# Context products of a cross-attention: one value matrix against 256 tokens in four column groups, and a 0/1 matrix back to token rows

## The reference

```python
q = split(x @ Wq + bq); k = split(ctx @ Wk + bk); v = split(ctx @ Wv + bv)   # 16 heads of 8 features
scores = q @ k.T / sqrt(8)            # 77 columns for each token and head
keep the 32 largest scores of each row; w = softmax over what is kept
out = concat(w @ v) @ Wo + bo
```

## Time and profile before

| what | us |
|---|---|
| runs | 611.84, 613.88, 619.55 |
| profiled execution, its own time | 621.08 |
| its span from first to last instruction | 619.3 |
| TE busy | 542.8 |
| VectorE busy | 409.9 |
| ScalarE busy | 294.3 |
| GpSimd busy | 223.5 |
| mean granted clock of TE, as a share of full | 0.964 |

### The profile page before, as it was taken

One profiled execution on the slowest core, in us unless ns is written; L12 is line 12 of the kernel. 1 busy time (PEld: TensorE's weight loads), 2 busy tenths in 40 slices (PEclk: granted clock), 3 DMA queues, 4 the chain that ended last, 5 costly groups with the idle time before them and its releaser, 6 DMA issues.

```text
span 619.3 us, 12159 instructions
## 1 busy us (share of the span) xinstructions
PE 542.8 (88%) x3982; PEld 425.0 (69%) x3982; DVE 409.9 (66%) x2225; ACT 294.3 (48%) x726; POOL 223.5 (36%) x227
## 2 busy tenths in 40 slices
PE   4888679997899899989998889968799988999997
PEld 2565347875667566768667656657577877989997
DVE  3566765533544598776697998876768889534643
ACT  2342314324775576663763645545575555222221
POOL 4016830002433464562552655542623432420000
PEclk9997989998999999998999979889899999789999
DMA  4500102404000000000000000003600000000000
GB/s 132 177 1 14 45 20 68 130 25 153 2 2 1 0 2 2 2 1 1 2 2 1 2 3 2 1 1 103 190 11 11 13 19 19 22 23 1 26 1 10
DMA packets 23050, 19.17 MB, mean 31 GB/s; under 512 B 2048, under 2 KB 18508, under 8 KB 22989
## 3 DMA queue, kind: packets, MB, share of 16 engines
q1 hardware_dynamic: 22477, 17.36, 9.2%
q0 software_dynamic: 512, 1.05, 0.6%
HBM read 15.38 MB, written 3.01 MB: 30 GB/s over the span
## 4 chain that ended last, share of the span: by engine, by line
PE 60%; DVE 23%; ACT 10%; issue 4%; POOL 1%; another core or an unknown queue 1%; DMA 1%; DVEq 0%; ACTq 0%
PE ps L1793 51%; DVE wk L1165 6%; DVE top L1155 4%; PE ps L2183 3%; DVE nmax L1101 3%; ACT prT L1562 2%; DVE sel_mem L994 2%; ACT w_mem L1555 2%; PE ps L2245 1%; ACT pr L1555 1%; ACT w_lo L1681 1%; DVE xn L1128 1%; PE ps L2366 1%; DVE sel_mem L1289 1%; PE ps L1805 1%
## 5 line engine op out<-in xcount | busy, mean ns | idle before, releaser
L1165 DVE MATCH_REPLACE8 wk<-top,wk 128x77 f32<-128x77 f32 x384 | 80.6, 225 | 0.8 <-issue 0.8
L1101 DVE TENSOR_REDUCE nmax<-ps 128x2 f32<-128x256 f32 (+1 forms) x64 | 51.2, 821 | 41.3 <-PE ps L1793 39.5
L687 POOL TENSOR_TENSOR w_mem<-w_mem,rinv 128x256 f32<-128x256 f32 (+3 forms) x44 | 53.3, 1223 | 52.7 <-DVE rinv L1107 52.2
L1289 DVE TENSOR_TENSOR sel_mem<-gr,ps 128x512 f32<-128x512 f32 x47 | 32.3, 687 | 53.5 <-ACT gr L1736 52.6
L1155 DVE MAX8 top<-wk 128x8 f32<-128x77 f32 x384 | 58.3, 225 | 2.1 <-issue 0.9
L1736 ACT ACTIVATE gr<-ps 128x512 f32<-128x512 f32 x47 | 28.1, 598 | 61.2 <-PE ps L1793 61.2
L1793 PE MATMUL ps<-cat_mem 64*128 64x512 f32 (+7 forms) x272 | 54.4, 480 | 1.5 <-ACT cat_mem L1539 1.5
L716 POOL TENSOR_SCALAR wk<-wk 128x616 f32<-128x616 f32 x16 | 28.1, 1755 | 59.4 <-DVEq L1169 59.2
L1555 ACT ACTIVATE w_mem<-ps,nmax 128x128 f32<-128x128 f32 (+3 forms) x88 | 44.5, 519 | 10.0 <-DVE nmax L1101 9.9
L1793 PE MATMUL ps<-prT,cat_mem 128*64 128x128 f32 x640 | 44.2, 287 | 0.0
L611 POOL TENSOR_TENSOR rstd<-var_eps,minus_half 128x4 f32<-128x4 f32 x8 | 8.2, 1026 | 97.8 <-DVE var_eps L831 97.7
(11 more groups left out here) (346 smaller groups left out, 1369.0 us busy)
## 6 DMA issues: line engine op xcount, KB each, us to landing
w_mem<-in_L_ffn_W_dram SPq DMA_DIRECT2D x12, 256.0 KB, 3.1
f_mem<-in_L_ffn_Wg_dram SPq DMA_DIRECT2D x8, 256.0 KB, 2.7
f_mem<-in_L_ffn_Wu_dram SPq DMA_DIRECT2D x8, 256.0 KB, 3.0
f_mem<-in_L_ffn_Wd_dram SPq DMA_DIRECT2D x8, 256.0 KB, 3.6
sel_mem<-in_L_ffn_W_dram SPq DMA_DIRECT2D x4, 256.0 KB, 4.0
xs_dram<-zero SPq DMA_DIRECT2D x1, 960.0 KB, 6.1
ys_dram<-f_mem SPq DMA_DIRECT2D x15, 64.0 KB, 1.5
xs<-xs_dram SPq DMA_DIRECT2D x3, 256.0 KB, 3.1
```

Source lines behind the costliest of these rows:

```text
L687: pool.tensor_tensor(pr[s][:, :, at:at + n], pr[s][:, :, at:at + n], rinv[:, i % 8, :].unsqueeze(2).to_broadcast([P, 2, n]), ALU.mult)\
L1101: dve.tensor_reduce(nmax[:, i % 8, :], ps[:, 2 * s:2 * s + 2, at:at + (c + 1) * P], X, ALU.max, negate=True).then_inc(nmax_ready, 1)
L1165: dve.match_replace(wk[q][:, t, h, :], top[q][:, t, h, 8 * r:8 * r + 8], src[:, t, h, :], GONE).then_inc(top_step, 1)
L1289: dve.tensor_tensor(hg[s][:, :], gr[s][:, :], ps[:, 2 * s + 1, :], ALU.mult)\
```

## The change

`context` puts the head's values on the stationary side: for each of the four heads one product, with 32 columns of `vh` (9 that count and 23 that belong to the next heads, or to a tail filled with ones) as the stationary operand and all 256 tokens of `pkT` as the moving one. The four outputs go to partitions 0 to 31, 32 to 63, 64 to 95 and 96 to 127 of the same 256 columns. A piece's result thus has its features on the partitions. ScalarE copies all 256 columns, to `cxT`. A new step `context_rows` brings a block's four pieces back to token rows: for each half and piece one product with `cxT` as the stationary operand and `pick9`, a 0/1 matrix of 36 columns which picks 9 of each 32 partitions, as the moving one. VectorE then normalises straight from PSUM. The fillers ahead of `context_T` are gone. `pkT` becomes one tile, and its two copies write strided. Two semaphores are merged. The transposes of the exponentials stay at their places in the order of every engine.

```diff
-        vh = sb("vh", [NC, B, HX, DX + 1])
+        vh_mem = sb("vh", [NC, B * HX * (DX + 1) + 32 - DX - 1])
+        vh = vh_mem[:, 0:B * HX * (DX + 1)].rearrange("p (b h d) -> p b h d", b=B, h=HX)
+        pick9 = sb("pick9", [P, 4 * (DX + 1)])
...
-        pkT = [part(sel_mem, t * S, 4, P)[0:NC] for t in range(2)]
-        cx = part(sel_mem, 2 * S, 2, 4, 8 * (DX + 1))
+        pkT = part(sel_mem, 0, 4, 2 * P)[0:NC]
...
+        cxT = [cxT_even, cxT_one, cxT_even, part(fn_flat[2], 0, 4, 2 * P)]
+        cn = [cn_first, cn_first] + [part(fn_flat[2], 2 * S, 2, D)] * 2
...
-            def context_norm(k):
-                dve.wait_ge(cx_ready, 4 * (k + 1))
+            def context_norm(k, bank):
+                dve.wait_ge(rows_cx_ps, k + 1)
...
-                act.activation(cx[:, n // 4 % 2, n % 4, :], ps[:, bank, 0:8 * (DX + 1)], ACT.Copy).then_inc(cx_ready, 1)
+                if n % 4 == 0 and n >= 8:
+                    act.wait_ge(rows_cx_ps, n // 4 - 1)
+                act.activation(cxT[n // 4][:, n % 4, :], ps[:, bank, 0:2 * P], ACT.Copy).then_inc(cx_ready, 1)
...
                 pe.wait_ge(pkT_ready, 2 * n + 2)
-                for t in range(2):
-                    for h in range(4):
-                        at = (4 * t + h) * (DX + 1)
-                        last = mm(ps[:, bank, at:at + DX + 1], pkT[t][:, h, :], vh[:, n // 8, 4 * (n % 4) + h, :])
+                for h in range(4):
+                    at = (HX * (n // 8) + 4 * (n % 4) + h) * (DX + 1)
+                    last = mm(ps[32 * h:32 * h + 32, bank, 0:2 * P], vh_mem[:, at:at + 32], pkT[:, h, :])
                 last.then_inc(cx_ps, 1)
                 return ((cx_ready, n + 1),)
+
+            def context_rows(k, bank, *free):
+                for signal, count in free:
+                    pe.wait_ge(signal, count)
+                pe.wait_ge(cx_ready, 4 * (k + 1))
+                n9 = 4 * (DX + 1)
+                for t in range(2):
+                    for n in range(4):
+                        last = mm(ps[:, bank, (4 * t + n) * n9:(4 * t + n + 1) * n9], cxT[k][:, n, t * P:(t + 1) * P],
+                                  pick9[:, :])
+                last.then_inc(rows_cx_ps, 1)
+                return ((cn_ready, 2 * (k + 1)),)
 
             def context_T(k, out_c, *free):
...
-                if k < 2:
-                    keep_busy(7, 4)
                 pe.wait_ge(cn_ready, 2 * (k + 1))
...
+                for k in range(2):
+                    if U == OUT[k]:
+                        seven = context_rows(k, 7, *seven)
...
+                if j == 3:
+                    four = context_rows(2, 4, *four)
...
+                if i == 4:
+                    four = context_rows(3, 4, *four)
```

More of the change, by code:

```diff
@@ L497, in decoder @@
         yg = part(fn_flat[1], 0, 2 * TB, D)
+        cxT_even = part(sel_mem, 2 * S, 4, 2 * P)
+        cxT = [cxT_even, cxT_one, cxT_even, part(fn_flat[2], 0, 4, 2 * P)]
+        cn = [cn_first, cn_first] + [part(fn_flat[2], 2 * S, 2, D)] * 2
         SCALE0 = float(D) ** -0.5
@@ L632, in _ @@
                 pool.memset(cum[q][:, 0:E], 0.0).then_inc(pool_step, own.up())
-            pool.memset(vh[:, :, :, :], 1.0).then_inc(pool_step, own.up())
+            pool.memset(vh_mem[:, :], 1.0).then_inc(pool_step, own.up())
+            pool.memset(pick9[:, :], 0.0).then_inc(pool_step, own.up())
             pool.iota(slots[:, :], pattern=[[1, P]], base=0, channel_multiplier=0,
@@ L643, in _ @@
             keep_where(later_t16[:, :], [[-1, P]], 0, 1, NEG)
+            by_head = pick9[:, :].rearrange("p (h d) -> p h d", h=4)
+            pool.affine_select(out=by_head, in_=by_head, compare_op=ALU.not_equal, fill=1.0, base=0,
+                               pattern=[[-32, 4], [-1, DX + 1]], channel_multiplier=1).then_inc(pool_step, own.up())
             by_e = same_e16[:, :].rearrange("p (e j) -> p e j", e=E)
@@ L1603, in weights_T @@
                     act.wait_ge(cx_ps, n)
-                act.activation(pkT[t][:, :, :], tiles(bank)[0:NC], ACT.Copy).then_inc(pkT_ready, 1)
+                act.activation(pkT[:, :, t * P:(t + 1) * P], tiles(bank)[0:NC], ACT.Copy).then_inc(pkT_ready, 1)
             def tokens_high(k):
```

39 lines of the change are left out of this document (20 added, 19 removed).

## The result

The changed kernel takes 619.67 us (median of 20 runs, 614.59 to 623.84), the kernel before 613.60 (20 runs, 611.72 to 619.55). The ratio is 1.0073, 95% interval 1.0050 to 1.0096: slower by about 4.5 us, where 6.9 us faster was forecast. The sign was wrong, beyond what the measurement leaves open.

What follows compares the result with a forecast made beforehand. TE was taken as the bound in most stretches, VectorE in others. Gains 3.9 + 4.0 + 1.6 + 4.55 less losses 1.8 + 2.0 + 0.9 + 2.0 + 0.5 gave 6.85 us: 607 us from the median 613.88, range 598 to 621.

Steps and rivals of the forecast that it cites:

- contexts 0, 1, 2 and the clock behind 2: Self-attention: shorter contexts on TE gain 3.9 us; full clock after the third of them gains 1.7 us.
- unit 36: Block 0's `context_rows` in self-attention delays TE's transposes and next scores; fillers gone give part back: 0.9 us lost.
- the clock behind context 5: Self-attention: of a 6.8 us low-clock stretch, only the last 4 or so count; full clock gains 2.0 us.
- unit 44: Block 1's `context_rows`: score product waits for VectorE's normalisation; fillers gone and full clock help: 2.0 us lost, bounds 1 and 3.
- contexts 9, 10, 11: Weight preparation and tokens: TE's time counts, each context falling from 1.71 to 0.70 us to the next start.
- step 3: Block 2's `context_rows` among the experts: 1.7 us of products plus 0.3, the down product covering 1.14: 2.0 us lost.
- context 14: Tokens: this context runs at low clock, 2.97 us; the new one takes twice 0.70: 1.6 us gained.
- context 15, block 3, clock there: Last context shortened from 1.71 to 0.70 us; `context_rows` at step 4 loses 1.8; half the clock's 1.7, 0.85, gained.
- first rival: In the contexts, the four column groups run one after another, so contexts give 0.5 not 9.5: 616 us, chance 0.10.
- second rival: The clock doesn't care for thin products, so the 4.55 us of clock gain go: 611.5 us, chance 0.14.
- third rival: `context_rows` brings low clock at its four places, costing 10 us, and the 4.55 gain goes: 621.6 us, chance 0.13.
- clock term: Removing thin products keeps full clock after three contexts: 4.55 us gained, bounds 0 and 6.8.

Runs made afterwards that it cites:

- e0: The kernel before, unchanged, run again for a second reference trace: 614.39 us, ratio 0.998.
- e6: The kernel before with each 9-column context product widened to 126 columns, the same nine repeated: 613.02 us, ratio 0.9944.
- e2: The changed kernel with one product of 288 columns in place of the sixteen records of `context_rows`, waits kept: 609.49 us, ratio 0.9897.
- e14: The changed kernel with the ways back of blocks 0 and 1 moved later, block 2's left in place: 610.32 us, ratio 0.9931.
- e8: e4 with block 1 (contexts 4 to 7) put back in the old form: 606.00 us, ratio 0.9869.
- e11: The changed kernel with only block 2's products moved, from step 3 to the end of the step before: 623.14 us, ratio 1.0119.
- e12: The changed kernel with only block 0's way back moved late: products at the end of unit 36, normalisation and turn one unit later: 610.25 us, ratio 0.9930.
- e1: The changed kernel with the fillers put back ahead of the transposes in `context_T`, blocks 0 and 1: 620.69 us, ratio 1.0067.
- e3: The changed kernel, products moved: block 0 one unit earlier, block 1 to the end of unit 44, block 2 ahead of step 3: 616.67 us, ratio 1.0008.
- e10: The changed kernel with only block 1 moved: products at the end of unit 44, normalisation and turn one unit later: 617.82 us, ratio 1.0053.
- e4: e3 with block 0's products at the end of unit 36 instead, its normalisation and turn one unit later: 608.68 us, ratio 0.9881.
- e13: The changed kernel with blocks 1 and 2 moved as in e3, block 0 left in place: 617.78 us, ratio 1.0037.
- e9: e4 with each product with the 0/1 matrix streaming 108 columns in place of 36: 606.74 us, ratio 0.9866.
- e15: e8 with the remaining products with the 0/1 matrix streaming 108 columns in place of 36: 603.80 us, ratio 0.9853.

## Why the prediction was wrong

By its own terms, in us (gain negative), against the distances of the traces:

```
contexts 0, 1, 2 and the clock behind 2       -3.9 - 1.7            = -5.6    measured -5.0
unit 36 and the clock behind context 5        +0.9 - 2.0            = -1.1    measured +5.1
unit 44 to the experts                                                +2.0    measured +7.2
contexts 9, 10, 11                                                    -3.0    measured -2.0
step 3                                                                +2.0    measured +4.3
contexts 12, 13                                                        0      measured -0.85
context 14                                                            -1.6    measured -3.4
context 15, block 3, clock there              -1.0 + 1.8 - 0.85     = -0.05   measured +1.3
ScalarE's copies                                                      +0.5    within the rows above
sum                                                                   -6.85   measured +6.7
```

**Right.** The price of a context: 0.57 us to the next start, and the four groups side by side. The 0.70 taken among the experts, for a change of the array's mode, isn't borne out: it is 0.57 there too. The sorting was right for contexts 0 to 2. It was off by about 1 us each way elsewhere: context 9 brings the next weights' copy 1.0 us nearer (8.08 us behind w, e0 9.11), but ScalarE's copy of scores then waits 2.76 us where it waited 1.71, and nothing is left; contexts 12 and 13, priced at 0, gain 0.85 together.

The first rival is out: the eight records of a context started within 0.26 us. The prediction let the Trainium skill, "TensorE: Matmul & The Clock Gate", Part 3, speak for that rival. That was half the page: the same part gives three column tiles of 32 outputs a measured speedup of 2.38 times ("Measured speedup vs the span model"). The trace agrees with that table. It doesn't agree with the sentence that weight loads overlap only where the row group differs: the loads for the second records start at 388.30 to 388.32 us, while the first products run from 388.28 us on, in the same rows of the array.

The second rival is out too: in e6 nothing but the width of the products changed, and the mean clock rose from 0.963 to 0.975. The tie to idle gaps in the same page ("Why this matters for your kernels") doesn't cover the fall at context 2, where the trace has TE busy 3.08 of 3.40 us. At 338 us there is a gap ahead, but one of 1.69 us, shorter than those the page speaks of.

**Wrong, first: unit 36**, "0.9 lost", and "behind context 5: 2.0" gained. This is 6.2 of the 13.5 us between forecast and measurement. I priced the delay of TE's transposes and VectorE's wait of about 1 us; VectorE waited 2.22 and 2.56. Two things make it up. The place: with one product instead of sixteen (e2) 52 to 58 takes 40.36 us, and 37.4 with the late place and no low stretch in it (37.41 in e14, 37.38 in e8), so at least 3 us hang on standing between the scores' copy and the unit's transposes. The clock: the products ran at half speed and with them the units behind, two stretches of 6.8 us where before had one. From 40.36 to 45.93 are 5.6 us more, of which about 1.3 (1.87 less 0.59) is the longer series at full clock and some 4 the clock, by my estimate.

**Wrong, second: unit 44**, "2.0 lost; bounds 1 and 3". Measured 7.2. The wait for `cn` came as described (1.79 us), and the clock was missing. With the same code from maximum 62 to w, e11 and e12 have 13.7 us of low clock in that distance and take 35.69 and 36.33 us, the changed kernel has 20.5 and takes 38.38: about 0.35 us for each at half clock. The kernel before has 5.7 there. Taken down to that, the changed form would take about 33.2 us, 2.0 above before. That is an extrapolation over two points. It comes out at the forecast's wait term, which may be luck; the other 5 us would be the low clock that I had put down as a gain ("full clock in what follows").

**Wrong, third: step 3**, "2.0 lost", because "the down product covers 1.14 us". It covers TE's time, but VectorE's gating product is queued behind the normalisation and TE needs it next: an idle time of TE of 1.82 us that I had not looked for. 4.3 in all. At the end of step 2 (e11) the same products cost 2.5: 1.8 from w to g 4 and 0.7 from g 4 to g 6.

**The clock term as a whole** had the wrong sign: 4.55 us gained were forecast, and the mean clock went from about 0.963 to 0.961. The gain behind context 2 did come (a stretch of 3.4 us is worth 1.2 to 1.6), and one at context 14 that I hadn't counted; units 36 and 44 took it back. I took away four groups of thin products' low stretches and gave none to the new thin products, although the third rival said just that: "`context_rows` brings its own low clock", 621.6 us, with a chance of 0.13. Measured 619.67: this rival came, at two of the four places, which is the point I had named. What spoke "against" it, 36 columns in place of 9, was no evidence: the records take 279 ns with 36 columns (changed kernel) and 275 with 126 (e6), so the columns don't set their length. And those of units 36 and 44 stand behind a wait of TE, 1.69 and 0.81 us, which the old ones did not. That the rival's 621.6 us lies near is in part luck: it put 10 us on low clock at four places and took the waits as forecast, but the waits of unit 36 and step 3 were short as well.

**Better than forecast:** context 14, because the stretch at 526 us went altogether in that trace. It is back for 3.4 us in e1, e3 and others, which take 13.2 to 13.3 us there in place of 11.69; without the clock little of the 3.4 us is left.

**Still open:** what sets where a low stretch begins. e3, e10 and e4 have the same code from maximum 62 to w and 3.4, 10.2 and 17.1 us of low clock in it, with 31.40, 34.06 and 35.47 us (e13 and e14, also 10.2, take 34.11 and 33.80). What differs is what ran ahead. The traces don't say more, and so no placement's clock can be forecast from its own stretch alone.

The best versions beat both kernels: e8, e9 and e15 take 1.3 to 1.5% less than the kernel before, 604 to 607 us (four runs each). What they share is block 0's late place, and either the old form where VectorE covers the contexts anyway, or wider products.

## What to carry to other kernels

When a change replaces thin products by others that it adds elsewhere, price the added ones by the same clock rule that you credit for the removed ones, and look at what stands ahead of them: a wait followed by a series whose length its columns don't set was the worst place here. A way back that two engines must hand over goes where they wait least for each other (VectorE 1.87 us in e12, 4.78 in the changed kernel), and its consumer's first queued instruction must not be what the producer needs next. Here block 0's place alone was worth 7 to 10 us of a change whose gains in the traces were 11.2 (5.0, 2.0, 0.85 and 3.4). Compare traces by distances between common instructions and runs by time at equal clock: the spans alone hid all of this behind 7 us of spread.

## What the runs showed of the hardware

- Four products of 256 f32 columns on four column groups of 32 (8 records of about 380 ns) take 0.64 us from start to end, 0.57 to the next start. One product of 256 columns on the full array has 0.60 from start to end.
- With 128-column weights a product's time hardly depends on its columns up to 126: sixteen records of 9 columns take 1.85 to 1.95 us, of 36 columns 1.87 to 1.98, of 126 columns 1.95 to 2.05, at full clock.
- More columns can make a kernel faster: 126 in place of 9 raised the mean clock from 0.963 to 0.975 and gave 0.9944 of the time.
- Time follows the mean clock by 4.2 us per 0.01. If every slowed moment lay on the path, it would be 615 / 0.965 x 0.01 = 6.4; so about two thirds do, by estimate. A stretch of 3.4 us at 1.2 GHz adds 1.2 to 1.6 us.
